# A fused quantize, LoRA and matmul kernel: another order on ScalarE and in the transfer queue at the front of the program

## The reference, cut to what matters

```
x: (8, 256, 1024) float32
# 1. quantize: 8 thresholds, deltas and zero points; each |x| picks a group
gi = sum(|x|[..., None] <= thresholds); d, zp = deltas[gi], zeropoints[gi]
q  = where(gi == G, 0, (clip(round(x / d) + zp, 0, 63) - zp) * d)
# 2. four LoRA experts on q, gated by a softmax over the two best of four logits
x1 = x + sum_e gates[e] * (q @ A[e].T) @ B[e].T * 4
# 3. a linear layer with one of five adapters, chosen for each batch element
y  = x1 @ W.T + (x1 @ lora_A[label]) @ lora_B_w.T * 0.5
# 4. a second layer with mixed adapters (gate: 8 x 16) and a shared one
z  = y @ kernel + bias + adapters(y)
out = x1 + z
```

## Time and profile before

| | |
|---|---|
| median of 3 runs | 464.24 us (463.82 to 464.54) |
| the profiled execution | 463.36 us, its span 461.6 us |
| TensorE busy | 448.9 us, 97% of the span |
| VectorE busy | 392.6 us, 85% |
| ScalarE busy | 357.6 us, 77% |
| GpSimd busy | 9.3 us, 2% |
| HBM read, written | 39.5 MB, 10.5 MB |
| mean granted clock of TensorE | 0.989 |

### The profile page before, as it was taken

One profiled execution on the slowest core, in us unless ns is written; L12 is line 12 of the kernel. 1 busy time (PEld: TensorE's weight loads), 2 busy tenths in 40 slices (PEclk: granted clock), 3 DMA queues, 4 the chain that ended last, 5 costly groups with the idle time before them and its releaser, 6 DMA issues.

```text
span 461.6 us, 5629 instructions
## 1 busy us (share of the span) xinstructions
PE 448.9 (97%) x2166; PEld 350.3 (76%) x2166; DVE 392.6 (85%) x392; ACT 357.6 (77%) x296; POOL 9.3 (2%) x11
## 2 busy tenths in 40 slices
PE   8889599999999999999999999999999999999997
PEld 8767477888888887777877877787778777867884
DVE  1587499999889999999799999999996999899410
ACT  1459999974697989799799988789697899778002
POOL 0000001000010000000010000000000000000000
PEclk9899799999999999999999999999999999999999
DMA  7998436220444250325107108015215014101102
GB/s 248 342 353 348 93 80 177 75 57 1 110 154 147 92 109 29 114 92 159 57 1 250 58 1 236 15 59 159 98 51 159 1 58 138 50 9 45 47 1 91
DMA packets 36124, 50.35 MB, mean 109 GB/s; under 512 B 26658, under 2 KB 26914, under 8 KB 33826
## 3 DMA queue, kind: packets, MB, share of 16 engines
q1 hardware_dynamic: 35090, 42.66, 29.4%
q0 software_dynamic: 1008, 7.34, 4.8%
HBM read 39.51 MB, written 10.49 MB: 108 GB/s over the span
## 4 chain that ended last, share of the span: by engine, by line
PE 88%; ACT 4%; SPq 3%; DMA 3%; issue 1%; ACTq 0%
PE bank L1088 13%; PE bank L1090 13%; PE bank L1089 13%; PE bank L971 6%; PE bank L1065 6%; PE bank L999 6%; PE bank L1030 6%; PE bank L1025 6%; PE bank L1026 6%; PE bank L940 5%; DMA xq<-xt_in 3%; PE bank L1086 2%; PE bank L995 2%; ACT level L427 2%; PE bank L1006 1%
## 5 line engine op out<-in xcount | busy, mean ns | idle before, releaser
L680 DVE COPY_PREDICATED val<-inside,val 128x2048 f32<-128x2048 uint8 x56 | 142.5, 2546 | 0.3
L440 ACT ACTIVATE val<-level,shift,small 128x2048 f32<-128x2048 int16 x64 | 134.0, 2093 | 10.0 <-PE bank L971 9.9
L427 ACT ACTIVATE level<-xq,inv 128x2048 int16<-128x2048 f32 x64 | 127.9, 1998 | 5.6 <-DMA xq<-xt_in 5.1
L1088 PE MATMUL bank<-p_hi,x_hi 128*128 128x512 f32 x256 | 103.0, 402 | 0.0
L1090 PE MATMUL bank<-p_hi,x_lo 128*128 128x512 f32 x256 | 100.1, 391 | 0.0
L1089 PE MATMUL bank<-p_lo,x_hi 128*128 128x512 f32 x256 | 100.1, 391 | 0.0
L662 DVE TENSOR_SCALAR val<-val,width,unshift 128x2048 f32<-128x2048 f32 x64 | 87.0, 1359 | 6.4 <-ACT val L440 6.3
L671 DVE TENSOR_SCALAR inside<-absx,thr 128x2048 uint8<-128x2048 f32 x56 | 72.6, 1296 | 0.0
L1088 PEld LDWEIGHTS bank<-p_hi,x_hi 128*128 128x128 f32 x256 | 48.1, 188 | 17.6 <-issue 9.0
L1089 PEld LDWEIGHTS bank<-p_lo,x_hi 128*128 128x128 f32 x256 | 48.1, 188 | 10.5 <-issue 0.7
L1090 PEld LDWEIGHTS bank<-p_hi,x_lo 128*128 128x128 f32 x256 | 48.1, 188 | 10.5
(11 more groups left out here) (98 smaller groups left out, 449.9 us busy)
## 6 DMA issues: line engine op xcount, KB each, us to landing
xs<-xt_in SPq DMA_DIRECT2D x8, 1024.0 KB, 4.9
wst<-w_in SPq DMA_DIRECT2D x14, 512.0 KB, 4.2
xq<-xt_in POOLq DMA_DIRECT2D x7, 1024.0 KB, 6.9
out_t<-ost SPq DMA_DIRECT2D x14, 512.0 KB, 3.3
la<-la_in SPq DMA_DIRECT2D x4, 512.0 KB, 5.6
kst<-k_in SPq DMA_DIRECT2D x4, 512.0 KB, 12.9
lb<-lb_in SPq DMA_DIRECT2D x4, 512.0 KB, 15.3
kst<-k_in SPq DMA_DIRECT2D x1, 2048.0 KB, 10.4
```

The lines of the kernel that those rows point to most:

```text
L427: nc.scalar.activation(level[:, g % 2], xq[:, c % 2], ACT.Copy, scale=inv[:, group(g)]).then_inc(levels_made, 1)
L440: nc.scalar.activation(val[:, turn(c, g)], level[:, g % 2], ACT.Relu, bias=shift[:, group(g)], scale=par[:, 1, group(g)]).then_inc(raised, 1)
L680: nc.vector.copy_predicated(val[:, acc(c)], inside[:, g % 2], val[:, turn(c, g)]).then_inc(merged, 1)
L1088: mm(o, x_hi[:, s, k, at], p_hi[:, h, k], start=False, stop=False)
```

## The change

Five edits. (1) The queue of SyncE: `la[0]` comes in two halves with a semaphore each, `bw` goes ahead of `ab`, `wst[0]` ahead of all of `kst`, `xq` and `wst[1]` ahead of the label loads and `alt`. (2) TensorE opens with five rounds of ones, waits for each half of `la[0]` by itself, does two products of u_product(0) ahead of the first six k_updates, and the last two k_updates behind u_product(0); k_update(1, 7) moves from o = 4 to o = 6 of step 7. (3) ScalarE: weight_hi(0) comes right after the splitting of ab; u_out(0), p_out(0) and rows_out(0), (1) move ahead of magnitude(0); u_out(1) stands behind levels(0, 1), weight_hi(2) ahead of levels(0, 2); from step 1 on u_out comes before the step's groups. (4) VectorE: weight_lo(0) comes ahead of k_add. (5) TAKEN and LAGS: (0,2) is in step 1, step 2 has none, (0,3) and (0,4) are in step 3, and so one group fewer is done up to step 7 and one more in step 8; mid(0) is in step 7, mid(1) in step 14, and some gates, turns and copies move by one step.

```diff
--- before.py
+++ after.py
@@ -56,7 +56,7 @@
 TOP_K = 2.0
 ZSLOTS = 4
 KPARTS = 4
-WARM, WARMUPS = 256, 7
+WARM, WARMUPS = 256, 5
 LORA0 = 4.0
 LORA1 = 0.5
 
@@ -168,6 +168,7 @@
     k2_in, w_in, bet_in = sem("k2_in"), [sem("w_in0"), sem("w_in1")], sem("bet_in")
     bias_in, x_done = sem("bias_in"), sem("x_done")
     ones_made, bias_hi_made, bias_made, taken = sem("ones_made"), sem("bias_hi_made"), sem("bias_made"), sem("taken")
+    lora_first = [sem(f"lora_first{h}") for h in range(HALVES)]
     lora_in = [sem(f"lora_in{g}") for g in range(NG)]
     small_in, warm_made = sem("small_in"), sem("warm_made")
     k_part_in = [sem(f"k_part_in{i}") for i in range(KPARTS)]
@@ -213,8 +214,8 @@
 
 
     AHEAD = 2
-    LAGS = [(2, 4, 5, 6, 7, 9), (3, 3, 4, 5, 5, 6), (3, 4, 4, 5, 6, 7), (3, 5, 5, 6, 7, 9), (2, 5, 5, 6, 7, 8), (2, 3, 3, 3, 4, 5), (1, 2, 2, 4, 4, 5), (2, 2, 3, 3, 4, 6)]
-    TAKEN = [0, 0, 2, 2, 2, 2, 1, 1, 0, 1, 1, 1, 1, 1, 1, 1, 1, 2]
+    LAGS = [(2, 4, 5, 6, 7, 9), (2, 3, 3, 4, 4, 5), (3, 4, 4, 5, 6, 8), (3, 6, 6, 7, 8, 10), (2, 5, 5, 6, 8, 9), (2, 3, 3, 3, 4, 5), (1, 2, 2, 4, 4, 5), (2, 2, 3, 3, 4, 6)]
+    TAKEN = [0, 1, 0, 2, 2, 2, 1, 1, 1, 1, 1, 1, 1, 1, 1, 1, 1, 2]
     ORDER = [(c, g) for c in range(BATCH) for g in range(G)]
     SLOTS = STEPS + BATCH * KT
     LAST = STEPS + BATCH * KT - 8
@@ -309,24 +310,26 @@
         def _(sp):
             sp.dma_start(small, a["small"]).then_inc(small_in, 16)
             sp.dma_start(itok_sb, itok).then_inc(itok_in, 16)
-            for g in range(NG):
+            for h in range(HALVES):
+                at = slice(h * HALF, (h + 1) * HALF)
+                sp.dma_start(la[:, 0, at], a["la"][:, 0, at]).then_inc(lora_first[h], 16)
+            for g in range(1, NG):
                 sp.dma_start(la[:, g], a["la"][:, g]).then_inc(lora_in[g], 16)
+            sp.dma_start(bw, a["bw"]).then_inc(bw_in, 16)
             sp.dma_start(ab_raw, a["ab"]).then_inc(ab_in, 16)
-            sp.dma_start(bw, a["bw"]).then_inc(bw_in, 16)
+            sp.dma_start(wst[0], w_v[0]).then_inc(w_in[0], 16)
             for i in range(KPARTS):
-                if i == KPARTS // 2:
-                    sp.dma_start(wst[0], w_v[0]).then_inc(w_in[0], 16)
                 sp.dma_start(kst[:, i * KO:(i + 1) * KO], k_v[0, :, i * KO:(i + 1) * KO]).then_inc(k_part_in[i], 16)
             sp.dma_start(ident_raw, a["ident"]).then_inc(ident_in, 16)
             sp.dma_start(bdmask, a["bdmask"]).then_inc(bdmask_in, 16)
+            sp.dma_start(xq[:, 0], x_v[0]).then_inc(x_first_in, 16)
+            sp.dma_start(wst[1], w_v[1]).then_inc(w_in[1], 16)
             sp.wait_ge(itok_in, 16)
             label = [sp.value_load(itok_sb[0:1, b:b + 1], min_val=0, max_val=LAB - 1) for b in range(BATCH)]
             for b in range(BATCH):
 
                 sp.dma_start(alt[b % BG * R:(b % BG + 1) * R, b // BG],
                              a["alt"][bass.ds(label[b], 1)].rearrange("o r i -> (o r) i")).then_inc(alt_in, 16)
-            sp.dma_start(wst[1], w_v[1]).then_inc(w_in[1], 16)
-            sp.dma_start(xq[:, 0], x_v[0]).then_inc(x_first_in, 16)
             for g in range(NG):
                 sp.dma_start(lb[:, g], a["lb"][:, g]).then_inc(lb_in[g], 16)
             sp.dma_start(before, a["before"]).then_inc(before_in, 16)
@@ -459,8 +462,6 @@
 
             def kp_split(h):
                 for o in range(KT):
-                    if h == 0 and o == 4:
-                        weight_hi(0)
                     act.wait_ge(k_sum, h * KT + o + 1)
                     if h == 1 and o < KT - 1:
                         act.wait_ge(kp_read, o + 1)
@@ -553,6 +554,7 @@
             act.wait_ge(ab_in, 16)
             for part in AB_PARTS:
                 nc.scalar.activation(ab[(slice(None),) + part], ab_raw[(slice(None),) + part], ACT.Copy).then_inc(ab_hi_made, 1)
+            weight_hi(0)
             kp_split(0)
             bwp_hi()
             act.wait_ge(ident_in, 16)
@@ -564,28 +566,34 @@
                 nc.scalar.activation(ust[:, n % 2], ubank[n], ACT.Copy).then_inc(u_made, 1)
 
             act.wait_ge(tables, 1)
+            def p_out(n):
+                act.wait_ge(ofull, n + 1)
+                h, i = n // KT, tile_of(n)
+                nc.scalar.activation(p_hi[:, h, i], obank[n % RING], ACT.Copy).then_inc(p_hi_made, 1)
+
             levels(0, 0)
             raise_levels(0, 0)
             act.wait_ge(bwp_made, 1)
             weight_hi(1)
+            u_out(0)
+            p_out(0)
+            for i in range(HALVES):
+                rows_out(i)
             magnitude(0)
             levels(0, 1)
+            u_out(1)
             raise_levels(0, 1)
+            weight_hi(2)
             levels(0, 2)
-            def p_out(n):
-                act.wait_ge(ofull, n + 1)
-                h, i = n // KT, tile_of(n)
-                nc.scalar.activation(p_hi[:, h, i], obank[n % RING], ACT.Copy).then_inc(p_hi_made, 1)
-
             for n in range(STEPS):
 
                 if n > 1 and n + 1 < STEPS and n + 1 not in (KT, KT + 1):
                     weight_hi(load_of(n + 1))
-                if n == 1 or n == KT:
+                if n == KT:
                     u_out(n - 1)
-                if n:
+                if n > 1:
                     p_out(n - 1)
-                if 0 < n <= NG:
+                if 1 < n <= NG:
                     for i in range(HALVES):
                         rows_out((n - 1) * HALVES + i)
                 if n == KT - 1:
@@ -606,13 +614,9 @@
                 if n == 0:
                     for c, g in GROUPS[0]:
                         quant(c, g)
-                for c, g in GROUPS[n + 1][:1]:
-                    quant(c, g)
-                if 0 < n < KT - 1:
+                if 1 < n < KT - 1:
                     u_out(n)
-                if n == 1:
-                    weight_hi(load_of(n + 1))
-                for c, g in GROUPS[n + 1][1:]:
+                for c, g in GROUPS[n + 1]:
                     quant(c, g)
                 if n in EXP:
                     gate_exp(EXP[n])
@@ -724,8 +728,6 @@
                 if h:
                     dve.wait_ge(vfull, 1)
                 for o in range(KT):
-                    if h == 0 and o == 1:
-                        weight_lo(0)
                     dve.wait_ge(kp_hi_made, h * KT + o + 1)
                     nc.vector.tensor_tensor(kp_lo[:, o], kst[:, o], kp_hi[:, o].bitcast(F32), ALU.subtract).then_inc(kp_lo_made, 1)
 
@@ -809,6 +811,7 @@
 
             ab_lo(0)
             ab_lo(1)
+            weight_lo(0)
             for o in range(KT):
                 k_add(0, o)
             kp_lo_part(0)
@@ -914,8 +917,11 @@
                 last.then_inc(vfull, 1)
 
             for g in range(NG):
-                pe.wait_ge(lora_in[g], 16)
+                if g:
+                    pe.wait_ge(lora_in[g], 16)
                 for o in range(KT):
+                    if g == 0 and o * P % HALF == 0:
+                        pe.wait_ge(lora_first[o * P // HALF], 16)
                     at = o % 2 * BATCH * R + g * BATCH * RG
                     last = mm(obank[o // 2][:, at:at + BATCH * RG], la[:, g, o * P:(o + 1) * P], gm, start=True, stop=True)
                     if g == NG - 1 and o % 2:
@@ -928,15 +934,15 @@
                     pe.wait_ge(afree_late, o // 2 - KT // 4 + 1)
                 last = mm(cbank[:, 0:BATCH * R], bw[:, o], aefft[:, o], start=o == 0, stop=o == KT - 1)
             last.then_inc(cfull, 1)
-            pe.wait_ge(ab_lo_made, 2)
-            for o in range(KT):
-                k_update(0, o)
-
             def u_product(n):
                 pe.wait_ge(w_in[n % 2], 16 * (n // 2 + 1))
                 if n >= 2:
                     pe.wait_ge(u_made, n)
                 for o in range(KT):
+                    if n == 0 and o == 2:
+                        pe.wait_ge(ab_lo_made, 2)
+                        for k in range(len(kfirst)):
+                            k_update(0, k)
                     mm(ubank[n], wst[n % 2][:, o], aefft[:, o], start=o == 0, stop=False)
 
             def u_adapters(n):
@@ -1012,6 +1018,9 @@
                     u_product(n)
                     if n:
                         u_adapters(n)
+                    else:
+                        for k in range(len(kfirst), KT):
+                            k_update(0, k)
                 if n == KT - 1:
                     k_update(1, n - 1)
                 if h == 0 and n in MID:
@@ -1030,7 +1039,7 @@
                     last = mm(obank[n % RING], w_lo[side(n)][:, o], kp_hi[:, o], start=False, stop=o == KT - 1)
                     if n == KT - 1 and o < KT - 1:
                         last.then_inc(kp_read, 1)
-                    if n == KT - 1 and o == KT // 2:
+                    if n == KT - 1 and o == KT - 2:
                         k_update(1, n)
                 last.then_inc(ofull, 1)
                 if n == 0:
```

## The result

The changed kernel takes 459.99 us, the median of 16 runs from 455.21 to 462.52; the kernel before, on the same chip, 463.83 (463.06 to 465.02). Between the medians that is 3.8 us, or 0.8%, where 7.4 us were forecast. The ratio is 0.9887, 95% interval 0.9860 to 0.9913, or 1.1% faster: it leaves out one run that counts as slow (462.52) and is that of the means, 458.60 and 463.86. With two lots of runs mean and median differ. The kernel before has a spread of 2 us, this one of 7, in two lots: seven runs from 455.2 to 457.8 and nine from 459.8 to 462.5. The lower lot is where the forecast lay. The profiled execution (461.93 us, span 460.1) is from the upper one, and shows what went wrong there.

A forecast was written before the change was run, and what follows sets the result against it. From step 2 on TensorE's unbroken matmuls bound the kernel, so an earlier step 2 shortens it: 7.6 - 0.2 = 7.4 us, profiled 463.36 to 455.96, median 456.8; range 454.7 to 460.2, the forecast's own 456.0 to 457.6.

The forecast's parts named there:

- A: Rival, 2 in 10: clock falls in TensorE's new hole at 30.6 to 33.3, costing 1.7 to 2.2 us; 458.5 to 459.0.
- B: Rival, 1 in 10: VectorE or ScalarE becomes the bound in steps 8 to 14, costing 1 to 3 us; 457.8 to 459.8.
- 0.6 on top of 456.8: Opening DMA: a fixed 0.6 us per transfer, if exposed by splitting la[0], would put lb[0] at 33.9 and the time at 457.6.
- rival D: Slower, 0.8 in 10: u_out(0) waits for alt, each us after 32.4 delaying ScalarE and TensorE; alt at 41 gives 465.2.
- The walk of ScalarE and TensorE: Ahead of step 2: new order timed piece by piece; u_made 2 at 39.3, step 2 at 49.6 against 57.22, 7.6 us gained.
- This gain of some 2.3 us I count as nothing: Opening: step 0 starts at 24.7 instead of 27.04, counted as zero because TensorE then waits for alt and lb[0].
- the bound for the two rounds less: Opening: dropping two rounds of ones saves up to 0.9 us; L920 ends between 12.3 and 13.2, taken as 12.5.
- the splitting of la[0]: Opening: loading la[0] in halves priced at 0, since the DMA stream was full with pieces of 128 to 1024 KB.
- Alt at "near 32.0": Ahead of step 1: alt, now last before lb, lands near 32.0, at best 1.3 us earlier.
- Rival C: 1 in 10: alt and lb come early because the 240 GB/s stretch shrinks; up to 1.5 us more, 455.3.
- What lies between the start of step 1 and u_made 2 decides: ScalarE's new list brings u_made 2 by 39.3, 6.4 us of margin where TensorE had a 5.26 us hole.
- The later moves: Steps 8 to 14, changed TAKEN and mid steps: nothing gained, 0.2 us of loss booked, with 0 and 2 as ends.

The follow-up runs named there:

- a2: The changed kernel with seven opening rounds of ones instead of five, la[0] still in halves: 456.17 us, ratio 0.9869.
- a1: The changed kernel run once more, unaltered: 460.58 us, ratio 0.9933 to the kernel before.
- a4: The changed kernel with the whole old opening, la[0] as one transfer and seven rounds of ones: 456.67 us, ratio 0.9850.
- c2: a4 run a second time, unaltered: 456.61 us, ratio 0.9850.
- b3: a4 with ScalarE's list, TAKEN and LAGS put back as in the kernel before: 457.68 us, ratio 0.9866.
- b4: a4 with alt filled from la by two 512 KB transfers to 128 partitions, as a price and not a version: 453.95 us, ratio 0.9786.
- a3: The changed kernel with la[0] as one transfer again, still five rounds of ones: 455.97 us, ratio 0.9875.

## Why the prediction was partly right

**The direction, the range and the place: right.** 459.99 is in 454.7 to 460.2, at its end, and the whole gain lies ahead of step 2 with 404.5 us behind it. That it is inside is partly luck: the upper end was set by rivals A and B, holes in other places, and the second series of the same kernel has its median, 460.58, outside. The forecast's own range, 456.0 to 457.6, missed the median by 2.4 us. Two side sums are 0.2 off: 0.6 on top of 456.8 is 457.4 and not 457.6, and rival D at 41 comes to 465.4.

**The walk of ScalarE and TensorE: right, where the opening is undisturbed.** In a2 alt was there at 31.67 (32.0 forecast), lb[0] at 32.72 (33.3), ust of step 1 at 38.75 (38.9), step 2 at 48.66 (49.6). Step 0 began at 25.55 (24.7), after a hole of 2.01 us for kp_lo that the prediction has in its times but does not name as a hole; in six of the ten profiles with a hole of 1.9 us or more there, the clock fell behind it.

**The step that failed is the opening**, with "This gain of some 2.3 us I count as nothing" and, ahead of it, the bound for the two rounds less: "nothing is gained if the first half of la[0] comes no earlier than the whole did". I took a start that is earlier to be a gain or nothing, and asked only for the first piece. The pieces behind it were the question. In the kernel before, la[1] took 5.2 us from its issue at 2.0, so it was there at 7.2, and L920, begun at 5.87 with 1.83 us for a piece, wanted it at 7.7: half a microsecond in hand. By the prediction's own price the new opening takes 0.9 away and, with one issue more in the queue, sends la[1] 0.43 later. A hole of some 0.8 us was thus to be had from the trace of before. The DMA issues of la[1], of before, after, a1 and a2, in this order (transfer, count, KB, us to landing):

```profile
la<-la_in SPq DMA_DIRECT2D x1, 512.0 KB, 5.2
la<-la_in SPq DMA_DIRECT2D x1, 512.0 KB, 6.6
la<-la_in SPq DMA_DIRECT2D x1, 512.0 KB, 5.6
la<-la_in SPq DMA_DIRECT2D x1, 512.0 KB, 4.7
```

In a1 TensorE was early: it began L926 at 5.05 and wanted la[1] at 6.94. In the profile after it was not: the five rounds took 4.63 us, it began at 5.62 and wanted la[1] at 7.75, as before, and the hole of 1.29 us is there because la[1] landed 1.8 us later, at 9.0. So the second term that was put at nothing, the splitting of la[0], belongs to the failed step. Its price was taken from the earlier trace rows, a stretch from 13.20 on, and not from the queue's first 10 us. In the eight profiles with la[0] whole la[1] landed at 6.9 to 7.4, in the four with halves at 6.9 to 9.0, and the queue moved 362 to 408 GB/s from 5 to 9 us in the eight, 313 to 371 in the four; that points to the halves as the reason, but doesn't show it. What both together cost is some 4 us, since in half the executions the clock falls (by the inference above) and then stays low through L926 and L935, and the DMA cover that I counted on was only 2.7 us deep.

**Rival A had the mechanism, for one of three holes.** It gave the fall of the clock to the wait for alt and lb (2 in 10, 1.7 to 2.2 us). That fall exists too: in all four profiles in which TensorE waited more than 1 us for alt (a1 4.45, a4 2.84, c2 2.20, b3 1.31) the clock fell in that hole or behind it, so 2 in 10 was too low. The dearer fall is the one behind the hole for la, 13.6 us at half clock in the profile after; a1's L926 has the hole with no fall.

**Alt at "near 32.0"** was one execution's stream taken for all. Alt landed at 31.7 in a2, 35.1 in a4, 36.2 in a1. Its lateness isn't explained: the same transfers, in the same order, at 264 and 254 GB/s in the windows 26 to 30 of a2 and 197 and 229 in a1. It isn't alt's alone, for xq, issued ahead of it, was there at 25.4 in a2 and 28.9 in a1. That it is the form of alt's transfers which makes the stretch slow is shown (b4); what makes it slower in one execution than in another is open. Rival C's claim, more to gain if the slow stretch shrinks, was shown as a price, some 3 us of the median.

**Where the gain comes from** was put wrong: "What lies between the start of step 1 and u_made 2 decides" credits the list. The queue with TensorE's and VectorE's order alone brings 6.2 us, the list alone 4.5, both with the old opening 6.6 (a4) and 6.7 (c2). They fill the same hole; xq 7 us earlier moves all of ScalarE's work, and the old list fits into it: in b3 ust ends at 45.5, u_product(2) starts at 46.85 (and would have been due at 45.7 by the walk, so the old list is about as long as it may be). Walking the old list with the new xq would have told that.

**The later moves** cost nothing that shows: no wait of TensorE behind 60 us in the profile after (booked 0.2; c = 0 and 1 in new steps, the margins as walked).

## What to carry to other kernels

An engine that is made to start earlier uses up the margin of every transfer behind its first one, and a first load in pieces puts one more issue ahead of them: before cutting filler work or splitting a first load, put the landing time of each following piece beside the time it is wanted, and ask what the clock does if one is late. When a change has two parts that fill the same hole, walk each alone; and when a copy or a transfer order looks like a sure gain, look at the spread of the runs as well as at the median, as a kernel that hangs on a transfer with no margin falls into two lots.

## What was not expected of the hardware

- After a hole of 1.29 us in a run of L926, matmuls of 64 columns back to back, the granted clock went to 0.50 at 9.5 us and stayed there for 9.5 us although TensorE was busy without a gap; it came back at 23.1, 4 us into L935 (256 columns). In a2 the same L926 without a hole kept 1.00 for all of its 7.25 us. In a1, with a hole of 1.1 us, it kept it too. So nearly the same hole had either outcome.
- The hole ahead of step 0 had either outcome too: of 1.91 to 2.07 us in eight profiles, it was followed by some 3.5 us of half clock in four (after, a3, c2, b4) and by none in the other four (a1, a2, a4, b3).
- The seven rounds of ones, 14 records, took between 4.81 us (before) and 5.87 (b3), and L920 begins up to 1.0 us later or earlier with it. The view gives the granted clock as 1.00 in all of this time, so it doesn't show why.
- While eight transfers of 128 KB to 32 partitions each are under way, the queue moves 197 to 264 GB/s with all DMA engines shown busy (a1, a2); with two of 512 KB to 128 partitions in their place, 410 to 422 (b4).
